# Silu from PSUM, two additions on TensorE, one input block on VectorE, and a new order of the steps, in a fused scan, attention and feed-forward kernel

## The reference

```python
# layer 0: group norm, then a selective scan with 192 inner channels and 16 states
xz = u @ in_proj_w.T;  xm, z = split(xz)                 # 192 and 192 channels
xm = silu(causal_conv(xm, taps=4) + conv_b)
dt, Bm, Cm = split(xm @ x_proj_w.T)                      # 6, 16, 16
delta = softplus(dt @ dt_proj_w.T + dt_proj_b)
h = exp(delta*A) * h + delta * Bm * xm                   # per channel, state and point in time
y = (sum over states of h*Cm + xm*D) * silu(z)
x = x + layernorm(y @ out_proj_w.T) * gamma + beta
# layer 1: linear attention (no softmax), then a feed-forward part in rounded fp8 / fp16
t = t + attn(ln(t));  t = t + ffn(ln(t))                 # 96 -> 384 -> 96, relu
```

## Time and profile before

| | before |
|---|---|
| median of 3 runs | 2680.51 us |
| lowest and highest run | 2678.12 and 2680.65 us |
| profiled execution, span | 2683.3 us |
| POOL busy | 2576.9 us (96%), 654 instructions |
| DVE busy | 2603.7 us (97%), 2503 instructions |
| ACT busy | 2392.7 us (89%), 3971 instructions |
| PE busy | 2196.6 us (82%), 9844 matmuls |
| DMA, mean busy share of 16 engines | 55.1% on the main queue |
| granted TensorE clock, mean | 0.910 |

### The profile page before, as it was taken

One profiled execution on the slowest core, in us unless ns is written; L12 is line 12 of the kernel. 1 busy time (PEld: TensorE's weight loads), 2 busy tenths in 40 slices (PEclk: granted clock), 3 DMA queues, 4 the chain that ended last, 5 costly groups with the idle time before them and its releaser, 6 DMA issues.

```text
span 2683.3 us, 34179 instructions
## 1 busy us (share of the span) xinstructions
PE 2196.6 (82%) x9844; PEld 788.6 (29%) x9844; DVE 2603.7 (97%) x2503; ACT 2392.7 (89%) x3971; POOL 2576.9 (96%) x654
## 2 busy tenths in 40 slices
PE   6677777888888888888888888888888888888878
PEld 3222223323323323323323323323323322322323
DVE  7999999999999999999999999999999999999996
ACT  5677777999999999999999999999999999999976
POOL 4999999999999999999999999999999999999991
PEclk8788888889889899899989999899989989989978
DMA  6455555555555555555555556556556555555533
GB/s 247 157 176 167 172 173 175 185 184 193 197 185 188 202 184 193 197 185 196 194 185 205 184 188 199 187 190 205 183 191 199 185 192 192 177 194 194 169 124 79
DMA packets 171161, 494.44 MB, mean 184 GB/s; under 512 B 23040, under 2 KB 44672, under 8 KB 154144
## 3 DMA queue, kind: packets, MB, share of 16 engines
q1 hardware_dynamic: 170976, 492.25, 55.1%
HBM read 400.28 MB, written 91.88 MB: 183 GB/s over the span
## 4 chain that ended last, share of the span: by engine, by line
POOL 54%; issue 28%; DVE 11%; PE 3%; ACT 2%; DMA 1%; SPq 0%; POOLq 0%; DVEq 0%; ACTq 0%
POOL R L651 35%; POOL D L640 15%; DVE R L1194 7%; POOL du L633 4%; DVE D L1178 2%; ACT DA L824 1%; PE G L1430 1%; DMA R<-ths 1%; PE Y L1507 0%; PE G L1464 0%; DVE yv L1215 0%; ACT dl L796 0%; PE PB L1430 0%; DMA ds<-lo_d 0%; DVE G L1219 0%
## 5 line engine op out<-in xcount | busy, mean ns | idle before, releaser
L1194 DVE TENSOR_TENSOR_SCAN R<-DA,R,D 128x512 f32<-128x512 f32 x1344 | 1642.0, 1263 | 18.3 <-ACT DA L824 18.2
L651 POOL TENSOR_TENSOR R<-R,Cs 128x2048 f32<-128x2048 f32 x383 | 1593.3, 4187 | 0.0
L824 ACT ACTIVATE DA<-ds,kept_w 128x512 f32<-128x512 f32 x1536 | 1049.6, 687 | 198.7 <-DVE R L1194 183.5
L640 POOL TENSOR_TENSOR D<-us,Bs 128x2048 f32<-128x2048 f32 x193 | 877.6, 4547 | 15.4 <-DVE R L1194 7.8
L1178 DVE TENSOR_TENSOR D<-us,PB 128x2048 f32<-128x2048 f32 x191 | 431.4, 2259 | 5.8 <-ACT PB L810 5.6
L1507 PE MATMUL Y<-R,kept_w 128*32 128x512 f32 x2048 | 301.0, 674 | 43.8 <-POOL R L651 43.8
L1464 PE MATMUL G<-un,wcv 96*128 96x512 f32 x512 | 262.4, 660 | 20.5 <-ACT rs L835 10.7
L1511 PE MATMUL Y<-R,kept_w 128*32 128x256 f32 x2048 | 147.1, 407 | 100.2 <-POOL R L651 99.6
L1194 DVE TENSOR_TENSOR_SCAN R<-DA,D 128x512 f32<-128x512 f32 x192 | 222.4, 1203 | 4.6 <-ACT DA L824 4.6
L1430 PE MATMUL G<-sq,kept_w 96*96 96x512 f32 (+1 forms) x256 | 156.7, 697 | 78.9 <-ACT h L887 48.6
L1467 PE MATMUL G<-un,wcv 96*64 96x256 f32 x1024 | 173.0, 469 | 0.0
(11 more groups left out here) (223 smaller groups left out, 3217.7 us busy)
## 6 DMA issues: line engine op xcount, KB each, us to landing
Bs<-bc_d SPq DMA_DIRECT2D x128, 512.0 KB, 4.3
us<-lo_d SPq DMA_DIRECT2D x64, 1024.0 KB, 6.8
ds<-lo_d SPq DMA_DIRECT2D x64, 1024.0 KB, 7.2
Cs<-bc_d SPq DMA_DIRECT2D x128, 512.0 KB, 4.9
us<-hi_d SPq DMA_DIRECT2D x64, 512.0 KB, 6.4
ds<-hi_d SPq DMA_DIRECT2D x64, 512.0 KB, 5.1
lo_d<-dl SPq DMA_DIRECT2D x64, 256.0 KB, 2.0
lo_d<-du SPq DMA_DIRECT2D x64, 256.0 KB, 2.0
```

What stands on the lines that cost most here:

```text
L640: nc.gpsimd.tensor_tensor(shaped(D[:, s % NDBU, :, :], s), low(us, s) if s in LOWS else high(us), of_states(Bs, s), ALU.mult).then_inc(don ...
L651: nc.gpsimd.tensor_tensor(shaped(R[:, s, :, 0:T], s), shaped(R[:, s, :, 1:S], s), of_states(Cs, s), ALU.mult).then_inc(hc_done.sem, 1)
L824: nc.scalar.activation(DA[j % NDA][:, :], ds[:, i, :], ACT.Exp, scale=A[:, j:j + 1]).then_inc(exp_done.sem, 1)
L1194: nc.vector.tensor_tensor_scan(R[:, s, q, 1:S], DA[j % NDA][:, :], D[:, s % NDBU, q, :], before, ALU.mult, ALU.add).then_inc(scanned.sem, 1)
```

## The change

**Silu from PSUM.** `front_evac`, `raw` and the semaphore `front_ev` are gone. The front's four results stay in PSUM until `silu` of the next step reads them there: u from G3 and from the first half of G1, z from G2 and from the second half of G1, four ACTIVATE instructions instead of two.

```diff
-            def silu_u(k, after=None):
-                act.wait_ge(front_ev.sem, front_ev.at(k, after))
+            def silu(k, *src):
+
                 act.wait_ge(skipped.sem, skipped.at(k - 2))
                 act.wait_ge(du_done.sem, du_done.at(k - 2))
-                nc.scalar.activation(u[:, place(k) % 2, :], raw[:, 0, :], ACT.Silu).then_inc(silued.sem, 1)
...
+                for v in range(2):
+                    act.wait_ge(front_mm.sem, front_mm.at(k, FRONT[v]))
+                    nc.scalar.activation(u[:, place(k) % 2, part(v)], src[v], ACT.Silu, bias=cb[:, v:v + 1])\
+                        .then_inc(silued.sem, 1)
                 if there(k - ZS):
                     act.wait_ge(gated.sem, gated.at(k - ZS))
-                nc.scalar.activation(z[:, k % ZS, :], raw[:, 1, :], ACT.Silu).then_inc(silued.sem, 1)
+                for v in range(2):
+                    act.wait_ge(front_mm.sem, front_mm.at(k, FRONT[2 + v]))
+                    nc.scalar.activation(z[:, k % ZS, part(v)], src[2 + v], ACT.Silu).then_inc(silued.sem, 1)
                 nc.scalar.preload_act_table_set(EXP_LN)
```

```diff
+            def add_x(k, o):
+                pe.wait_ge(post_dve.sem, post_dve.at(k, 1))
+                pe.wait_ge(xq_in, count(k, 16, 16))
+                mm(o[0:C, :], idbet, xq[:, :], start=False, stop=True, skip_group_check=True).then_inc(x1_sum.sem, 1)
...
+            def x2_feed(m, o):
+                pe.wait_ge(f_yb.sem, f_yb.at(m))
+                mm(o[0:C, :], id16[:, :], y16[:, :], start=False, stop=True).then_inc(f_x2.sem, 1)
...
+            def keep_x1(k, src):
+                act.wait_ge(x1_sum.sem, x1_sum.at(k))
+                nc.scalar.copy(x1, src[0:C, :]).then_inc(x1_done.sem, 1)
...
+            def result(m, src):
+                act.wait_ge(f_x2.sem, f_x2.at(m))
+                nc.scalar.copy(x1_of(m), src[0:C, :]).then_inc(f_out.sem, 1)
```

```diff
+                if s == SHARED:
+                    nc.gpsimd.tensor_tensor(D[:, s % NDBU, 0:2, :], us[:, QUAD:QUADS, :],
+                                            Bs[:, 1, 0, :].unsqueeze(1).to_broadcast([128, 2, T]),
+                                            ALU.mult).then_inc(done, 1)
+                    nc.gpsimd.tensor_tensor(D[:, s % NDBU, 2, :], us[:, QUAD, :], Bs[:, 1, 1, :], ALU.mult).then_inc(done, 1)
+                    return
...
+            def shared_input(k):
+                dve.wait_ge(scanned.sem, scanned.at(k, QUAD * (SHARED + 1 - NDBU)))
+                dve.wait_ge(b_put.sem, b_put.at(k, BY_DVE[3]))
+                dve.wait_ge(u_in[1], count(k, 16, 16))
+                nc.vector.tensor_tensor(D[:, SHARED % NDBU, 3, :], us[:, QUAD + 1, :], PB[:, :], ALU.mult)\
+                    .then_inc(dbu_d.sem, 1)
```

**The order of the steps** is new on every engine. One line of ScalarE's list stands for it:

```diff
+                if there(g + 1) and g > 0:
+                    silu(g + 1, G3[:, :], G1[:, 0:H], G2[:, :], G1[:, H:T])
```

More of the change, by code:

```diff
@@ L661, in iteration @@
                     product(g, 0)
-                    inputs(g, 4)
+                    product(g, 1)
                 if there(g + 1):
@@ L911, in iteration @@
                     put_b(g, 1)
-                    decay(g, 0, 1)
-                if there(g + 1) and g > 0:
-                    front_evac(g + 1, 3, G1)
                 if there(g - 2):
@@ L935, in iteration @@
                 if there(g):
+                    decay(g, 1, 1)
+                if there(g - 2):
+                    token_copy(g - 2, G2)
+                if there(g):
+                    decay(g, 1, 2)
+                if there(g + 1):
+                    state_rows(g + 1, G3)
+                if there(g):
                     decay(g, 1, 3)
+                if place(g + 3) == 0 and later(g + 3):
+                    group_scale(g + 3, PB, 1)
                 if inside(g - 11):
@@ L955, in iteration @@
                     put_b(g, 3)
+                if place(g + 3) == 0 and later(g + 3):
+                    group_scale(g + 3, PB, 2)
+                if ahead(g + 11):
+                    chunk_mean(g + 11)
+                if there(g):
                     decay(g, 2, 3)
@@ L1322, in iteration @@
                     inputs(g, 3)
+                if place(g - 9) == 0 and early(g - 9):
+                    fold(g - 9, 1, G0)
+                if there(g):
                     scan(g, 2, 3)
@@ L1710, in iteration @@
+                if there(g - 1):
+                    (freed(f_ln, g - 10) or (place(g - 9) == 0 and freed(fold_ev, g - 9, 1))
+                     or freed(dl_done, g + 1))
+                    centre(g - 1, G0)
                 if there(g):
```

429 lines of the change are left out of this document (199 added, 230 removed).

## The result

| | before | after |
|---|---|---|
| median of 4 runs of each, side by side | 2679.32 us | 2753.66 us |
| lowest and highest | 2676.87 and 2680.65 us | 2750.69 and 2757.92 us |
| ratio, 95% interval | | 1.0273 [1.0256, 1.029] |
| profiled execution, span | 2683.3 us | 2751.5 us |
| granted TensorE clock, mean | 0.910 | 0.882 |

The changed kernel is 2.7% slower, 24 us over the 2730 that was forecast and inside the range of 2694 to 2760. The direction and the place of the wait are right. That the size is nearly right is in part luck: the wait that was forecast brings a good half of the time by which a step is longer than 39.3 us, and a second one, which belongs to a rival with a chance of 0.10, goes with the rest.

A forecast was written before the change was run, and what follows sets the result against it. POOL and DVE together bound the kernel, at about 40 us a step. Steps of 41.0 us: 52 x (41.0 - 40.14) adds 45 us, ten early steps 5, ends 0; 2733 profiled, 2730 as median, range 2694 to 2760.

The forecast's parts named there:

- the wait that was forecast: VectorE idle ahead of block 3 of quad 4 in every step, 1.0 to 2.7 us, taken as 1.7.
- POOL's part: POOL's inputs for quad 5 change from 4.547 to 2.36 and 1.27 us; its work falls by 0.9 to 39.2 us.
- DVE's part: VectorE loses two additions and gains one block; its work falls by 0.63 us to 39.3 us a step.
- If nothing else waited: Case "faster": steps of 39.3 us with the full relief, about 2632 us; chance of faster 0.34.
- ACT's part: ScalarE's work stays at 38.2 us a step; its stretch from table load to decay grows from 4.19 to 4.8 us.
- The layout of the step: Times from the start of scan (g,0,0): `variance_x2` ends 19.5, `scale_out` 21.9, q8 24.3; clock falls 21.2 to 24.6, returns 28.0 to 31.4.
- The formula for the end of the chain: TensorE's queue behind q8, at half clock until time r, ends at r + 4.6 - (r - 24.3)/2: 30.8 to 32.5.
- The size: Forecast step of 41.0 us against 40.14 before, with 1.7 us taken for VectorE's wait.
- rival (c): Clock also falls at the step's turn, second `gate` 2 to 3 us late: 42 to 43.5 us a step; chance 0.10.
- The early steps and the ends: Ten early steps go from 40.51 to 41.0 us, +5 us in all; start and end 0 +/- 5.
- The rule against the trace: The skill's rule on longer idle gaps, by which TensorE's clock stays up and the time is that of case "faster".
- What was to show it: Signs: ScalarE's largest TensorE wait at `inv_ln`, 1 to 2.5 us; VectorE idle before quad 4; clock falls each step; POOL idle.

The follow-up runs named there:

- e6: The kernel of e5 with POOL again making all four blocks of quad 5's input in one operation, VectorE's block left out: 2680.44 us.
- e5: The changed kernel with six unread matmuls around `add_x` and `variance(g-1, 1)` ahead of the first two taps of `conv`: 2631.27 us.
- e12: The kernel of e9 with six unread matmuls added, four behind `centre` where the sum had stood and two behind `add_x`: 2630.08 us.
- e11: The kernel of e2 with VectorE's `gate(g-1, 0)` moved ahead of `scan(g, 0, 0)` and `token_norm`: 2682.49 us.
- e2: The changed kernel with six matmuls whose result nobody reads put around `add_x` on TensorE, except in steps with a fold: 2666.79 us.
- e4: The changed kernel with `variance(g-1, 1)` moved ahead of the first two taps of `conv` on TensorE, nothing added: 2667.88 us.
- e7: The changed kernel with six unread matmuls a step in front of `x_proj`, where TensorE is dense: 2856.13 us.
- e3: The changed kernel with VectorE's `gate(g-1, 0)` ahead of `scan(g, 0, 0)` and TensorE's `sum_states(g-1, 4)` ahead of `x2_tokens`, no work added: 2770.83 us.
- e9: The changed kernel with `sum_states(g, 0)` moved from behind `centre` to ahead of `add_x`, and `variance(g-1, 1)` early as in e4: 2771.5 us.

## Why the prediction was right, point by point

**POOL's part: right.** 2.36 and 1.27 us a step were computed, 2.360 and 1.266 measured. e6 puts the worth of it at 0.65 us a step (40.10 less 39.45, e5's in its slowest execution), 49 us between the medians.

**DVE's part: right.** 39.3 us a step were computed; e12, with DVE full, takes 39.27. "If nothing else waited" was 2632; e5 and e12 give 2631 and 2630. The relief of both engines is real, and in the changed kernel all of it is lost in waits that begin at TensorE.

**ACT's part: right in that it bounds nothing, one term too high.** The stretch from table load to decay was put at 4.8 us. In e11's rows above it takes 4.41 (1611.00 to 1615.41), in the kernel after 4.42, against 4.19 before: cutting u and z in two costs 0.1 us each, not 0.3.

**The layout of the step: right, to 0.2 us.** With t = 0 at 1479.9 in the common step, `variance_x2` ends at 19.6 (19.5 computed), `scale_out` at 21.9 (21.9), q8 at 24.2 (24.3); the clock falls at 22.3 (21.2 to 24.6) and returns at 29.2 (28.0 to 31.4). The formula for the end of the chain, with r = 29.2, gives 31.35; `inv_ln` starts at 31.2. Of the 1.7 us that were taken for VectorE's idle time 1.19 are measured, within the 1.0 to 2.7. e2 and e4 confirm the two halves of the argument separately: e2, with e7 beside it, that the clock falls because the stretch is thin, e4 that a fall does most of its harm through the place of the variance in the queue. The loss needs both: either edit alone takes away 86 or 87 of the 122 us that the two together do.

**The size: right by two errors, which is luck.** A step of 41.0 was forecast and 41.43 measured, but the common one, which holds just the forecast wait, is 40.5 us (the mean of the six short ones of eight), so the wait that was forecast explains 1.2 of the 2.1 us over 39.3. The other 0.9 is a quarter of the 3.4 us by which the 42.7 and 45.2 us steps exceed the rest. The wait was put too high by 0.5 us (1.7 against 1.19), and what was left out made up for it. What was left out is rival (c), dismissed with "beside it PE is dense, which speaks against it": the clock does fall there, in two steps of eight, and the second `gate` then comes 3.08 us late, as the rival has it (2 to 3 us). The rival was wrong in its turn to let it fall in every step, and to make it depend on whether the idle time counts as thin: the same 1.68 us stand in the common steps without a fall.

Two conversions in the forecast don't follow from its own sum. At 62 steps, 41.6 us a step give 2767 us and not 2760, and rival (c)'s 42 to 43.5 give 2792 to 2885 and not 2765 to 2850. The measured 2753.66 lies inside the range either way.

**The early steps and the ends:** 40.71 measured (55.18 to 462.28 for ten), 41.0 forecast, +2 us instead of +5.

**The rule against the trace.** The Trainium skill, in "TensorE: Matmul & The Clock Gate", section "Why this matters for your kernels", names idle gaps between bursts of matmuls as the thing to avoid, longer than any that TensorE has in the changed kernel between 400 and 2500 us (2.36); by that rule alone that kernel should have run there at 2.4 GHz. The trace disagrees: the clock falls 67 times, after 2.33 us in the step shown, and in e5, where only 0.55 and 0.49 us of idle time are left in the same place, the clock stays up.

**What was to show it** was all there: ScalarE's largest wait for TensorE at `inv_ln`, VectorE idle ahead of block 3 of quad 4, one fall a step while TensorE waits for `scale_out` and q8, idle time on POOL.

**Left open:** why falls at the turn come in two steps of eight, where the wait is no longer than in the others, and why they vanish in e4, where nothing at the turn was altered. That the falls at the turn make the long steps long is read from the timeline, and from e2 and e4, where steps without such a fall are short; the run that was to test it by itself, e3, changed too much else. Open too is how much of e7's loss belongs to each of its waits.

## What to carry to other kernels

When the two fullest engines are relieved, lay out the order of the third over one step and ask where it runs thin before a queue on which others wait: the relief is worth only what that queue leaves of it. Put the instruction that is waited for at the head of the queue (e4) before trying to hold the clock; both together gave back all of it. Moving work into a thin stretch is no gain if it had covered a round trip where it stood (e9).
